# A corner of the decay tile is cleared by a minimum before the scores are multiplied in, instead of by a predicated copy after it

## The reference

```python
D = jnp.exp(log_D - max_log_D)
qk = jnp.einsum('bhsd,bhtd->bhst', qh, kh) / jnp.sqrt(jnp.asarray(dh, q.dtype))
C = qk * D
normalizer = jnp.maximum(jnp.abs(C.sum(-1, keepdims=True)), jnp.exp(-max_log_D))
Cn = C / (normalizer + EPS)
h = jnp.einsum('bhst,bhtd->bhsd', Cn, vh)
```

## Time and profile before

| | before |
|---|---|
| median of 3 runs | 800.06 us (799.39 to 800.25) |
| the profiled execution's own time | 801.35 us |
| its span | 799.6 us |
| busy share of the span: PE, DVE, ACT, POOL | 85%, 67%, 51%, 49% |
| attention stage | about 104 to 313 us of the span |
| chain that ended last | PE 49% of the span, most of it in the mixture stage (L1215 30%, L1233 14%) |

### The profile page before, as it was taken

The page is one execution under the profiler, slowest core; times in us unless marked ns, Lnnn a source line. Parts: engine busy times, 40 slices in busy tenths (PEclk is TensorE's granted clock), DMA queues, the critical chain, the costliest instruction groups (busy, mean ns, idle before and its releaser), DMA issues.

```text
span 799.6 us, 20108 instructions
## 1 busy us (share of the span) xinstructions
PE 682.2 (85%) x7280; PEld 595.1 (74%) x7280; DVE 536.7 (67%) x1056; ACT 411.7 (51%) x848; POOL 391.0 (49%) x595
## 2 busy tenths in 40 slices
PE   0876068888888882799999999999999999999994
PEld 0553057767677772688889998999998999999993
DVE  4762849899899997776427788533557666676750
ACT  0667246676766763554444232222556666656652
POOL 2111347888888884322112525123237575757554
PEclk9989559999999997799999999999999999999998
DMA  8883274644545512477752313233568797888854
GB/s 252 268 273 102 90 204 148 187 135 148 180 121 171 157 47 68 159 274 265 252 207 74 103 58 85 74 93 107 175 224 224 229 237 244 232 253 222 258 130 53
DMA packets 90720, 135.57 MB, mean 170 GB/s; under 512 B 16720, under 2 KB 44112, under 8 KB 90672
## 3 DMA queue, kind: packets, MB, share of 16 engines
q1 hardware_dynamic: 74128, 107.41, 40.8%
q0 software_dynamic: 7168, 17.04, 10.8%
q10 hardware_dynamic: 9376, 10.49, 4.2%
HBM read 92.32 MB, written 34.21 MB: 158 GB/s over the span
## 4 chain that ended last, share of the span: by engine, by line
PE 49%; DVE 4%; DMA 2%; POOL 2%; issue 1%; ACT 1%; POOLq 0%; ACTq 0%; DVEq 0%
PE psH L1215 30%; PE psY L1233 14%; PE psR L1260 2%; PE psT L1195 2%; DMA out<-ystage,sidx 1%; POOL out L1722 1%; PE psT L1268 1%; DMA xrows<-xn,eidx 1%; DVE w13l L1466 1%; DVE xnorm L1633 1%; PE psG L1275 1%; DVE xl L1454 1%; DVE stats L1524 1%; DVE over13h L1633 1%; ACT over13l L1402 0%
## 5 line engine op out<-in xcount | busy, mean ns | idle before, releaser
L1215 PE MATMUL psH<-xh,w13h 128*128 128x256 f32 (+1 forms) x768 | 222.8, 290 | 3.0 <-DVE w13l L1466 3.0
L1215 PE MATMUL psH<-xh,w13l 128*128 128x256 f32 (+1 forms) x768 | 216.6, 282 | 0.0
L1215 PE MATMUL psH<-xl,w13h 128*128 128x256 f32 (+1 forms) x768 | 216.0, 281 | 0.0
L1690 POOL TENSOR_TENSOR hl<-sg,hh 128x256 fp32r<-128x256 f32 (+1 forms) x96 | 79.5, 840 | 207.2 <-ACT hh L1334 206.5
L1215 PEld LDWEIGHTS psH<-xh,w13h 128*128 128x128 f32 (+1 forms) x768 | 138.5, 180 | 12.5 <-issue 7.7
L1215 PEld LDWEIGHTS psH<-xl,w13h 128*128 128x128 f32 (+1 forms) x768 | 138.9, 181 | 0.7
L1215 PEld LDWEIGHTS psH<-xh,w13l 128*128 128x128 f32 (+1 forms) x768 | 138.8, 181 | 0.0
L1460 DVE TENSOR_TENSOR sg<-sg,psH 128x256 f32<-128x256 f32 (+1 forms) x96 | 40.0, 417 | 98.3 <-ACT sg L1329 98.0
L1329 ACT ACTIVATE sg<-psH 128x256 f32<-128x256 f32 (+1 forms) x96 | 36.3, 378 | 130.8 <-PE psH L1215 126.1
L730 ACT ACTIVATE dec<-ring 128x512 f32<-128x512 f32 x128 | 73.8, 591 | 25.2 <-PE ring L634 24.8
L806 DVE SCALAR_TENSOR_TENSOR dec<-psQ,dec 128x512 f32<-128x512 f32 x128 | 79.3, 680 | 7.4 <-PE psQ L646 6.4
(11 more groups left out here) (226 smaller groups left out, 1381.8 us busy)
## 6 DMA issues: line engine op xcount, KB each, us to landing
raw<-w13T SPq DMA_DIRECT2D x64, 352.0 KB, 4.1
gcT<-ctxT ACTq DMA_DIRECT2D x8, 1024.0 KB, 6.5
kT<-ctxT SPq DMA_DIRECT2D x16, 512.0 KB, 5.2
ctxs<-ctx SPq DMA_DIRECT2D x16, 512.0 KB, 3.4
xn<-xnorm SPq DMA_DIRECT2D x16, 512.0 KB, 4.4
out<-xres SPq DMA_DIRECT2D x16, 512.0 KB
raw<-w2T SPq DMA_DIRECT2D x16, 512.0 KB
qst<-qT_all SPq DMA_DIRECT2D x14, 512.0 KB, 6.1
```

The source lines that it names most:

```text
L1215: last = nc.tensor.matmul(psH[m][0:n, v, :], w[wp][:, c, col:col + n], x[xp][:, c, :], start=(c == 0 and k == 0), stop=(c == DC - 1 and k ...
L1690: nc.gpsimd.tensor_tensor(hs[u.p][1][0:n, m, :], sg[0:n, m, :], hs[u.p][0][0:n, m, :].bitcast(F32), ALU.subtract).then_inc(hl_ready, 1)
```

## The change

Before, `clear` ran once in a step, after the four `weigh` of the step: it waited for them, ran a product of one column on a tile `none`, and then copied zeros to the corner of all 16 heads where the mask tile `corner` is 1. PE's `values` waited for the semaphore `cleared`.

Now `corner` holds 3.0e38 where the decay stays and 0 in the corner, and `clear` takes the minimum of the decay and `corner` in place, for 8 heads at a time (two groups of four, k and k+1). It runs ahead of the first and ahead of the third `weigh`, waits for ACT's exponentials of both groups, and DVE waits for the minimum itself (`link`) before it goes on. The tile `none`, the tile `zeros`, their two memsets on POOL and the semaphore `cleared` are gone.

```diff
-            c.link(nc.gpsimd.memset(g.none[:, :], 0.0))
-            c.link(nc.gpsimd.memset(g.zeros[:, :], 0.0))
-            c.link(nc.gpsimd.memset(g.corner[:, :], 0.0))
+            c.link(nc.gpsimd.memset(g.corner[:, :], 3.0e38))
...
-                pe.wait_ge(cleared, 4 * i + r + 1)
...
-            def clear(i, r):
+            def clear(i, r, k, use):
 
                 c, lo = r % 2, P - 32
-                dve.wait_ge(c_done, 16 * i + 4 * r + 4)
-                nc.vector.tensor_tensor(g.none[:, 0:1], g.none[:, 1:2], g.none[:, 2:3], ALU.mult)
-                wide = lambda t: t[lo:P, :].rearrange("p (o t) -> p o t", o=1).broadcast_to([32, NH, P - SPARE])
-                nc.vector.copy_predicated(dec[c][lo:P, :, :, SPARE:P].rearrange("p k g t -> p (k g) t"),
-                                          wide(g.corner).bitcast(U32), wide(g.zeros)).then_inc(cleared, 1)
+                dve.wait_ge(emptied, use + 1)
+                ends = dec[c][lo:P, k:k + 2, :, SPARE:P].rearrange("p k g t -> p (k g) t")
+                wide = g.corner[lo:P, :].rearrange("p (o t) -> p o t", o=1).broadcast_to([32, NH // 2, P - SPARE])
+                c_.link(nc.vector.tensor_tensor(ends, ends, wide, ALU.min))
...
                 for k in range(4):
+                    if k % 2 == 0:
+                        clear(i, r, k, decay_use(i, r, k + 1))
                     weigh(i, r, k, decay_use(i, r, k))
-                clear(i, r)
...
-            run(dve, c_, 4, step, drain)
+            run(dve, c_, 12, step, drain)
```

More of the change, by code:

```diff
@@ L102, in _ @@
                                            base=0, pattern=[[-1, P]], channel_multiplier=1))
-            c.link(nc.gpsimd.memset(g.none[:, :], 0.0))
-            c.link(nc.gpsimd.memset(g.zeros[:, :], 0.0))
-            c.link(nc.gpsimd.memset(g.corner[:, :], 0.0))
+            c.link(nc.gpsimd.memset(g.corner[:, :], 3.0e38))
             c.link(nc.gpsimd.affine_select(out=g.corner[:, :], in_=g.corner[:, :], compare_op=ALU.is_ge,
-                                           fill=1.0, base=SPARE, pattern=[[1, P - SPARE]], channel_multiplier=-1))
+                                           fill=0.0, base=SPARE, pattern=[[1, P - SPARE]], channel_multiplier=-1))
             c.link(nc.gpsimd.memset(g.before[:, :], 1.0))
@@ L523, in attention_stage @@
         (filled, emptied, v_ready, qk_done, c_done, inter_done, back_done, sq_ready, o_taken, red_done, ve_ready,
-         x_done, t_ready, kk_ready, qsc_ready, state_zero, weights_set, y_ready, state_done, state_taken, cleared, chain, pch, ach) = map(
+         x_done, t_ready, kk_ready, qsc_ready, state_zero, weights_set, y_ready, state_done, state_taken, chain, pch, ach) = map(
             a.sem, ["at_" + n for n in (
@@ L527, in attention_stage @@
                 "red_done", "ve_ready", "x_done", "t_ready", "kk_ready", "qsc_ready", "state_zero", "weights_set", "y_ready", "state_done",
-                "state_taken", "cleared", "chain",
+                "state_taken", "chain",
                 "pool", "act")])
@@ L805, in weigh @@
                 dk = dec[c][:, k, :, :].rearrange("p a t -> p (a t)")
-                weighed = nc.vector.scalar_tensor_tensor(out=dk, in0=psQ[:, k, :], scalar=SCALE, in1=dk, op0=ALU.mult, op1=ALU.mult)
-                weighed.then_inc(c_done, 1)
-            def clear(i, r):
+                nc.vector.scalar_tensor_tensor(out=dk, in0=psQ[:, k, :], scalar=SCALE, in1=dk,
+                                               op0=ALU.mult, op1=ALU.mult).then_inc(c_done, 1)
+            def clear(i, r, k, use):
                 c, lo = r % 2, P - 32
-                dve.wait_ge(c_done, 16 * i + 4 * r + 4)
-                nc.vector.tensor_tensor(g.none[:, 0:1], g.none[:, 1:2], g.none[:, 2:3], ALU.mult)
-                wide = lambda t: t[lo:P, :].rearrange("p (o t) -> p o t", o=1).broadcast_to([32, NH, P - SPARE])
-                nc.vector.copy_predicated(dec[c][lo:P, :, :, SPARE:P].rearrange("p k g t -> p (k g) t"),
-                                          wide(g.corner).bitcast(U32), wide(g.zeros)).then_inc(cleared, 1)
+                dve.wait_ge(emptied, use + 1)
+                ends = dec[c][lo:P, k:k + 2, :, SPARE:P].rearrange("p k g t -> p (k g) t")
+                wide = g.corner[lo:P, :].rearrange("p (o t) -> p o t", o=1).broadcast_to([32, NH // 2, P - SPARE])
+                c_.link(nc.vector.tensor_tensor(ends, ends, wide, ALU.min))
             def take(i, r):
@@ L1822, in build @@
             g.corner = c.sb("corner", [P, P - SPARE])
-            g.zeros = c.sb("zeros", [P, P - SPARE])
-            g.none = c.sb("none", [P, 4])
             with ExitStack() as gates:
```

## The result

The changed kernel takes 819.27 us (median of 4 runs, 817.47 to 821.71) against 799.77 us before: 2.5% slower, ratio 1.0246, 95% interval 1.0218 to 1.0273. The forecast was 816 us, its range 807 to 825. The profiled execution took 821.71 us with a span of 819.6, 20.0 more than the span before.

A forecast was written before the change was run, and what follows sets the result against it. A cycle through all four engines, 12.19 and 12.33 us per two steps, was taken as the bound. 2.07 us a round over 7.5 rounds, 15.5 us, plus 0.5 for the stage's start, gave 816 us, range 807 to 825.

The forecast's parts named there:

- `clear` isn't in the cycle: DVE's clearing stands behind the fourth `weigh`, outside the cycle through four engines; removing it counted for nothing in the total.
- only the first and third step count: In the second and fourth step `weigh` ends before PE begins `queries`, so minima added there cost nothing.
- The wait for the pair: Ahead of the first and third `weigh`, waiting for the second exponential of a pair costs nothing.
- The price of a minimum: On DVE ahead of `weigh`: 0.40 us each with gaps and wait, 0.80 per step, bounds 0.62 to 0.96.
- The stand in the third step: The third step's second minimum stands behind POOL's L904, begun 0.28 us before it: 0.57 us more.
- The first step's minimum: The first step's second minimum meets the end of POOL's L895 and gets in before L904; cost about 0.05 us.
- more stands: Rival: in the first step POOL's L904 goes ahead of the minimum; 3.07 us a round, 823 us; chance 0.13.
- The sum: Per round of four steps: 2 x 0.80, less 0.15, plus 0.05 and 0.57, 2.07 us; over 7.5 rounds 15.5 us.
- The term for what lies around the loop: Attention stage outside the full rounds: 0.5 us for the stage's start, and half a round.
- One cycle: In the attention loop one cycle through all four engines, once in two steps, sets the time: 12.19 and 12.33 us.
- Faster, since DVE is the busiest: Rival: DVE's own queue bounds the step; 0.29 us less a step, 9 us over 31 steps, 791 us; chance 0.10.

The follow-up runs named there:

- r odd alone: Kernel before with the minimum only in the steps with r odd, the predicated copy kept in the steps with r even; 824.45 us, ratio 1.0282.
- the second try at a better order: Changed kernel with DVE's step reordered: two products, second minimum, residual sum, two products, `take`, next step's first minimum; 821.94 us, ratio 1.0284.

## Why the prediction was right, point by point

- **That `clear` isn't in the cycle.** Right but for one place: without it the kernel gains 0.13 us a round, where the sum had nothing. The prediction had seen that PE's `gather_state` waits for `take`, and counted it only for a rival; in the second step that wait was real, and worth 0.17.
- **That only the first and third step count.** Right: 0.35 us a round for the minima of the other two, 3.25 for these; in the changed kernel `queries` waits in these two alone.
- **The wait for the pair.** Right, 800.24.
- **The price of a minimum.** Its own 0.20 was near the 0.22 taken, but the term for the wait behind it (0.04, or 0.07 with register instructions) was too small: 0.23 behind the first and 0.12 behind the second. The pair costs 0.55 + 0.43 = 0.98 us, not 0.80, which is just past the upper bound of 0.96.
- **The stand in the third step.** Right in kind; 0.46 in place of 0.57, since the minimum came 0.42 into L901 and not 0.28. The first step's minimum was forecast to meet POOL at the change of two instructions, at a price of 0.05. It met it there, and paid nothing; with r odd alone, at the same meeting, it paid 0.88. The precedent that the forecast leaned on, L813 at 205.45, didn't settle it, and this part of the forecast was luck: with the tie lost the whole change would have come near the 823 of the rival "more stands", as r odd alone did with 824.45.
- **The sum.** With the measured terms: 2 x 0.98 - 0.15 + 0.46 = 2.27 a round, measured 2.32. Seven rounds are 16.2 us. The term for what lies around the loop was mis-sized: 0.5 us and half a round were taken, about 1.5, and it is 3.3, of which 2.1 lie before the loop's first residual sum. There the minima wait for exponentials and stand behind POOL as well, and the second `queries` of the stage starts 1.46 us later, counted from the start of the stage. A term that the forecast didn't have comes on top: TensorE's granted clock is 0.50 at the start of the stage and rises to 1.00, twice that, about 13.1 us into it before and 16.6 us into it after. The first `values` (L660, L663 of before) falls into the difference and takes 1.94 us in place of 1.29. Why the clock rises later no run isolates; PE was waiting for the products in between. So the mechanism was right and the sizes short: 16.0 us were forecast for the stage and 19.55 came, and the number held its range with the help of the tie.
- **One cycle.** Here the argument was too narrow. It was right for work that is added, since the longer cycle decides. It would have been wrong for work taken away: as far as the timeline shows, a second cycle of the same length through PE and ACT takes over at once, and my later expectations for cutting the first one failed by this.
- **Faster, since DVE is the busiest.** DVE's busy time in a round fell by 1.3 us and the round grew by 2.3.

## What to carry to other kernels

Where four engines wait for one another in a ring, ask of each instruction whether it stands between two waits of the ring or behind them, before asking how long it takes: here four small instructions cost 0.35, or 2.4 to 3.25 us a round by their place. Measure all rings before forecasting a gain; when two are a tie, adding to one is paid nearly in full (2.32 us of 2.4 here), and cutting one was worth 0.08 us. And a DVE instruction whose inputs all lie in SBUF can cost its own time, or nearly that of a whole GpSimd instruction as well, by a hundredth of a microsecond: 0.20 or 1.08 us here. Last, where a change makes TensorE wait longer, read its granted clock beside the waits: in three of these kernels it fell inside the loop, and in the two where rounds with and without a fall compare, it lengthened a round by 1.2 us.

## What the runs showed that I had not expected

- A tie between DVE and POOL goes either way: with the same start to 0.01 us the minimum took 0.20 in one kernel (POOL's instruction 1.08 in place of 1.01) and 1.08 in another, in five rounds each. Within each of these traces the outcome of a tie is the same every time. The Trainium skill ("SBUF — State Buffer", the section on the two separate sides of SBUF) has whichever starts first hold the shared ports for its whole instruction. The minima of 0.66 and 1.08 agree: each ends 0.07 after POOL's instruction.
- A wait of DVE for its own last instruction is not free. In the second try at a better order the residual sum, which doesn't wait for the minimum, starts 0.03 us behind it:

```profile
205.47 0.20 DVE L813 TENSOR_TENSOR dec<-dec,corner 32x48 f32<-32x48 f32 x1
205.70 0.69 DVE L839 TENSOR_TENSOR xres<-xres,numc 128x512 f32 x1
```

  A product that waits for it starts 0.12 to 0.24 after its end. So by these rows the wait costs 0.09 to 0.21, more behind the first minimum of a step, where one more register instruction stands, than behind the second. The Trainium skill ("VectorE: DVE Perf Modes", the section on the DRAIN) says, of eight copies in a row, that a semaphore after each costs nothing extra. It doesn't hold for the minima of this kernel; the measurement decides.
